# Masks of an attention pass: POOL selects on the probabilities in place of matmuls on the scores, and the products of a unit one step later

## The chip, the core and the metric

One NeuronCore of one Trainium2 chip runs the whole program. The metric is the device time of one execution in microseconds (us), median of three runs. The engines are TensorE (PE; PEld is its weight load), VectorE (DVE), ScalarE (ACT), GpSimd (POOL) and SyncE (SP, which issues the DMAs). Each engine runs its own instructions in their written order, and semaphores connect the engines.

## The reference

Four images of 128 channels and 32 x 32 positions pass through three stages. Only the second, attention over 1024 tokens with 16 heads, is touched by the change:

```python
def _attn(q, k, v, mask=None):
    s = jnp.einsum('bhqd,bhkd->bhqk', q, k) / np.float32(np.sqrt(HD))
    if mask is not None:
        s = jnp.where(mask, s, jnp.float32(-1000000000.0))
    return jnp.einsum('bhqk,bhkd->bhqd', jax.nn.softmax(s, -1), v)
...
o1 = _attn(q, k1, v1, causal[None, None])
...
o2 = _attn(q, ks, vs)                       # 256 selected keys, no mask
...
winmask = causal & (ii[:, None] - ii[None, :] < WINDOW)   # WINDOW = 64
o3 = _attn(q, kw, vw, winmask[None, None])
g = gate[:, :, None, None, None]
o = g[:, 0] * o1 + g[:, 1] * o2 + g[:, 2] * o3
```

The first stage is a non-local block (its own attention, with no mask), the third a mixture of eight experts, two of them kept for a token. Everything is float32.

## The kernel before

The attention part (`attention_part`, `turns`) goes through the four batches one after the other. A batch has 8 **sides** of 2 heads each, so there are 32 sides. Each side does two things at once.

**The exact pass** computes transposed scores (keys on the partitions, queries along the row), their exponentials, and the products with the values. It is cut into 25 **units**, each one block of 128 keys against up to 512 queries, in six groups (`SUMS`): branch 1 (selected keys, no mask), branch 2 (window), branch 1, branch 2, branch 0 (causal), branch 0, for the lower and upper 512 queries in turn. Their widths, units 0 to 24: 512 512 | 192 192 192 128 | 512 512 | 64 192 192 192 128 | 512 384 256 128 | 512 512 512 512 512 384 256 128. For each unit and head:

- PE, `scores`: two float32r matmuls (L1285, L1293) into one of three PSUM banks. Between them stands a bf16 matmul of the identity with a table of 0 and -8e9 where a mask is needed: `causal_k` (L1288, 128 columns, 8 units of branch 0) and `window_k` (L1291, the width of the unit, all 9 units of branch 2). Per side that is 16 and 18 mask matmuls.
- ACT: Exp from the bank into `prob` (L1342), a ring of four units (`PROBS`). The row maximum has been subtracted already by an extra row of the matmul.
- PE, `products`: four matmuls 32 columns wide per head pair and kind, side by side in the array (L1314), into one of two sum banks.
- After the last unit of a group ACT copies the sum banks into `products` and `sums` (L1351, L1353: step `sum`).

**The division** comes once for every two sides: in the odd ones (and, for the last group, at the start of the next even one) DVE takes reciprocals of `sums` in halves of 256 columns (L1386), POOL multiplies (L1365) and for branch 2 also adds (L1368). After the two causal groups PE issues `proj` (L1256, L1257), which waits for POOL's results.

**The preparation** of the next side lies between the units: 40 `max0`, `max1`, `max2` steps (PE matmuls L1221 to L1242 into three spare banks, DVE reductions L1395, L1400) and a few transposes.

`exact_pass` and `window` write one order of steps for all engines; each engine takes its own steps from it. Scores of unit u are followed, at every even u, by the products of units u-2 and u-1. POOL has only the division steps; they stand in its queue in the same order.

Of the kernel before, what the change touches and what calls it, by code (L numbers as in the profile page):

```python
# [10 lines left out]
BF16 = mybir.dt.bfloat16  # L11
ALU = mybir.AluOpType
# [3 lines left out]
P = 128  # L16
# [8 lines left out]
HP = HG // 2  # L25
# [4 lines left out]
KEEP, WINDOW = 256, 64  # L30
SCALE = 1.0 / 8.0
NE, HID = 8, 341
WN = P + WINDOW
LNE, RMSE = 1e-5, 1e-6
MASKED = -8.0e9
# [896 lines left out]
UNITS = units()  # L932
LAST = [max(u for u, x in enumerate(UNITS) if x[:2] == k) for k in SUMS]
LOCAL = LAST[3] + 1
SCORES = 3
SPARES = 3
PIECES = 2
# [12 lines left out]
def exact_pass(w):  # L950


    todo, pieces = [], []
    if w % 2 == 0 and w > 0:
        pieces = [("divide", w - 1, len(SUMS) - 1, piece) for piece in range(PIECES)] + [("proj", w - 1, 1)]
    for u in range(len(UNITS) + 1):
        if u < len(UNITS):
            todo.append(("scores", w, u))
        ready = range(u - 2, u) if u >= 2 and u % 2 == 0 else range(u - 1, u) if u == len(UNITS) else ()
        for done in ready:  # L960
            todo.append(("products", w, done))
        for done in ready:
            if done in LAST:
                k = LAST.index(done)
                todo.append(("sum", w, k))
                if w % 2 == 1 and (k < len(SUMS) - 1 or w == NSIDE - 1):
                    pieces += [("divide", w, k, piece) for piece in range(PIECES)]
                    if SUMS[k][0] == 0:
                        pieces.append(("proj", w, SUMS[k][1]))
        todo += pieces[:1]  # L970
        pieces = pieces[1:]
    return todo + pieces
# [63 lines left out]
def attention_part(nc, d, ps, ident, eps, sb):  # L1036
    m = Mem()
    m.ps, m.ident = ps, ident
    m.ident_bf = sb("ident_bf", [P, P], BF16)
    m.causal_q = sb("causal_q", [P, P], BF16)  # L1040
    m.causal_k = sb("causal_k", [P, P], BF16)
    m.window_q0 = sb("window_q0", [P, WN], BF16)
    m.window_q = sb("window_q", [P, WN], BF16)
    m.window_k = sb("window_k", [P, WN], BF16)
    m.plain = sb("plain", [P, VD])
    m.wproj = sb("wproj_g", [P, NG, C])
    m.wvp = sb("wvp_g", [P, NG, C])
    m.small = sb("maxima", [P, 128])
    m.t2 = sb("t2a", [C, T])
    m.gates = sb("gates_a", [P, 3])  # L1050
    m.q1a, m.q1b, m.qa, m.qb, m.kwa, m.kwb = [sb(n + "_s", [P, 2, HP, T], F32R)
                                              for n in ("q1a", "q1b", "qa", "qb", "kwa", "kwb")]
    m.ksa, m.ksb = [sb(n + "_s", [P, 2, HP, KEEP], F32R) for n in ("ksa", "ksb")]
    m.k1a, m.k1b = [sb(n + "_s", [P, 2, T], F32R) for n in ("k1a", "k1b")]
    m.v1 = sb("v1_s", [P, 2, NT, KVR])
    m.vw = sb("vw_s", [P, 2, NT, NW])
    m.vs = sb("vs_s", [P, 2, KEEP // P, NW])
    m.products = sb("products", [P, 3, T])
    m.sums = sb("sums", [P, 3, T])
    m.prob = sb("prob", [P, PROBS, HP, CH])  # L1060
    m.mrows = sb("mrows", [HP * NT, 3, P])

    attention_constants(nc, m, d)
    turns(nc, m, OPENING, None, Kept(d, 0))
    every = {k: d[k] for k in ("qh", "kwh", "ksh", "vwh", "vsh", "k1ah", "k1bh", "v1h", "gatesh", "t2")}
    with nc.Fori(0, B - 1) as b:
        turns(nc, m, MIDDLE, Kept({k: x[0:B - 1] for k, x in every.items()}, b),
              Kept({k: x[1:B] for k, x in every.items()}, b))
    turns(nc, m, CLOSING, Kept(d, B - 1), None)


def attention_constants(nc, m, d):

    stack = ExitStack()
    s = open_sems(nc, stack, "c_load c_zero_dve c_zero_pool")
    consts = [(m.ident_bf[:], "ident_bf"), (m.causal_q[:], "causal_q"), (m.causal_k[:], "causal_k"),
              (m.window_q0[:], "window_q0"), (m.window_q[:], "window_q"), (m.window_k[:], "window_k")]
    consts += [(m.wproj[:, g], d["wproj_g"][g]) for g in range(NG)]
    consts += [(m.wvp[:, g], d["wvp"][g]) for g in range(NG)]
    with nc.Block() as block:  # L1080
        @block.sync
        def _(sp):
            for dst, name in consts:
                sp.dma_start(dst, d[name] if isinstance(name, str) else name).then_inc(s["c_load"], 16)
            sp.wait_ge(s["c_load"], 16 * len(consts))

        @block.vector
        def _(dve):
            dve.memset(m.plain[:], 1.0)
            dve.memset(m.small[:], -3.0e38)  # L1090
            for x in (m.q1b, m.qb):
                dve.memset(x[HD:P].bitcast(F32), 0.0)
            dve.memset(m.ksb[HD:P].bitcast(F32), 0.0).then_inc(s["c_zero_dve"], 1)
            dve.wait_ge(s["c_zero_dve"], 1)
            dve.memset(m.ksb[HD:HD + 1].bitcast(F32), 1.0)

        @block.gpsimd
        def _(pool):
            for x in (m.k1b, m.kwb):
                pool.memset(x[HD:P].bitcast(F32), 0.0).then_inc(s["c_zero_pool"], 1)  # L1100
            pool.wait_ge(s["c_zero_pool"], 2)
            pool.memset(m.k1b[HD:HD + 1].bitcast(F32), 1.0)
            pool.memset(m.kwb[WROW:WROW + 1].bitcast(F32), 1.0)
    phase_end(nc, s)
    stack.close()
# [6 lines left out]
def turns(nc, m, plan, cur, nxt):  # L1112
# [3 lines left out]
    ps = m.ps  # L1116
    stack = ExitStack()
    s = open_sems(nc, stack, "t2_loaded gates_loaded stored near0 near1 keys0 keys1 far0 far1 late0 late1 "
                             "rows0 rows1 rows2 fill_ready emptied scores_ready exp_done products_done "
                             "banks_free inverse_done divided o_done max_done")  # L1120
    negs = [m.small[:, k * HP * NT:(k + 1) * HP * NT] for k in range(3)]
    partial = m.small[:, 64:64 + HP * NT * 2].rearrange("p (h t a) -> p h t a", h=HP, t=NT)
# [6 lines left out]
    with nc.Block() as block:  # L1129
# [73 lines left out]
        def _(pe):  # L1203
# [56 lines left out]
            def scores(side, u):  # L1260
# [13 lines left out]
                for h in range(HP):  # L1274
# [8 lines left out]
                        pe.wait_ge(s["exp_done"], turn - SCORES + 1)  # L1283
                    bank = ps[:, turn % SCORES, 0:w]
                    pe.matmul(bank, kx, qx[:, k, h, q0:q0 + w], start=True, stop=False, skip_group_check=True)  # L1285
                    at = q0 - j * P
                    if br == 0 and at == 0:
                        pe.matmul(bank[:, 0:P], m.ident_bf[:], m.causal_k[:], start=False, stop=False,  # L1288
                                  skip_group_check=True)
                    if br == 2:  # L1290
                        pe.matmul(bank, m.ident_bf[:], m.window_k[:, at:at + w], start=False, stop=False,  # L1291
                                  skip_group_check=True)
                    pe.matmul(bank, ky, qy[:, k, h, q0:q0 + w], start=False, stop=True, skip_group_check=True)\  # L1293
                        .then_inc(s["scores_ready"], 1)

            def products(side, u):
# [2 lines left out]
                n = side * len(UNITS) + u  # L1299
                k = side * len(SUMS) + SUMS.index((br, c))  # L1300
                first = u == 0 or u - 1 in LAST
                pe.wait_ge(s["exp_done"], HP * (n + 1))
                if first and k >= 2:
                    pe.wait_ge(s["banks_free"], k - 1)
                if side > 0 or br == 0:
# [48 lines left out]

        @block.gpsimd
        def _(pool):
            for step in plan.of(("divide",)):
                _, side, k, piece = step
                br, c = SUMS[k]
                w = CH // PIECES  # L1360
# [494 lines left out]
```

## Time and profile before

| | |
|---|---|
| median of 3 runs (lowest to highest) | 3072.85 us (3072.46 to 3079.17) |
| the profiled execution's own time | 3068.73 us |
| its span in the trace | 3066.9 us |
| mean granted PE clock | 0.921 |
| busy: PE, DVE, ACT, POOL | 85%, 59%, 44%, 21% |

The span runs from the first to the last instruction. A granted clock of 1.00 is 2.4 GHz. Ends of matmuls are modelled in the trace, so the distance from one matmul's start to the next one's says more than its duration. The exact pass runs from 794 to 2545 us of the span; a side takes 52.7 to 53.0 us there where no new batch begins.

### The profile page before, as it was taken

Reading aid. Unit: us, or ns where it says so; the run is one execution under the profiler, and the core shown is the slowest. Engines: PE = TensorE matmul, PEld = TensorE weight load, DVE = VectorE, ACT = ScalarE, POOL = GpSimd, SP = SyncE. Lnnn points to the kernel's source line nnn. Section 1 sums busy time; section 2 is a strip of 40 time slices with the busy share of each in tenths; the row PEclk is TensorE's granted clock in tenths of the full one; section 3 lists DMA queues with packets and bytes.
Section 4 is the critical chain, followed back from the end, with each engine's and each line's share of the span. In section 5 each row is a group of like instructions: output and inputs, shape, how many; then the busy total and the mean of one; then the engine's idle time right before and its main releaser. Section 6 shows DMA issues by size and latency. Waiting matters only on the chain. (4 is left out here: it accounts for less than half of the span.)

```text
span 3066.9 us, 48595 instructions
## 1 busy us (share of the span) xinstructions
PE 2601.3 (85%) x17280; PEld 1736.8 (57%) x17280; DVE 1813.7 (59%) x3117; ACT 1364.7 (44%) x2816; POOL 635.5 (21%) x607
## 2 busy tenths in 40 slices
PE   5666577663899999899997999997999993998999
PEld 3544445343566665566664666665666652777777
DVE  4755658474466566466555556654656644766755
ACT  2323333231355554455553555553555453544544
POOL 0331405043011011011001001101101112544445
PEclk9777788776799999999998999999999995999999
DMA  2451706257755655546565565654655602000000
GB/s 88 171 195 68 293 27 267 75 216 226 151 120 126 126 105 115 131 102 137 107 130 111 107 130 117 135 117 98 135 117 121 131 3 102 4 18 7 17 11 8
DMA packets 191886, 342.32 MB, mean 112 GB/s; under 512 B 65632, under 2 KB 95040, under 8 KB 191152
## 3 DMA queue, kind: packets, MB, share of 16 engines
q1 hardware_dynamic: 191664, 339.49, 43.8%
q8 instruction: 124, 2.03, 0.3%
q14 instruction: 98, 0.80, 0.1%
HBM read 224.56 MB, written 112.99 MB: 110 GB/s over the span
## 5 line engine op out<-in xcount | busy, mean ns | idle before, releaser
L1342 ACT ACTIVATE prob<-ps 128x512 f32<-128x512 f32 (+5 forms) x1600 | 636.8, 441 | 740.0 <-PE ps L1293 586.1
L1395 DVE TENSOR_REDUCE maxima<-ps 128x1 f32<-128x512 f32 (+3 forms) x768 | 387.4, 547 | 297.6 <-PE ps L1224 149.6
L1314 PE MATMUL ps<-prob,plain 128*32 128x512 f32 (+5 forms) x3200 | 512.0, 443 | 0.0
L1365 POOL TENSOR_TENSOR products<-products,sums 128x256 f32<-128x256 f32 x192 | 140.6, 732 | 1609.0 <-DVE sums L1386 1607.7
L1400 DVE TENSOR_REDUCE maxima<-ps 128x2 f32<-128x512 f32 (+1 forms) x512 | 294.4, 607 | 244.1 <-PE ps L1242 108.6
L1386 DVE RECIPROCAL sums<-sums 128x256 f32<-128x256 f32 x192 | 331.5, 1736 | 104.0 <-ACT sums L1353 104.0
L1285 PE MATMUL ps<-q1a_s,k1a_s 128*128 128x512 f32 (+3 forms) x768 | 303.2, 395 | 0.0
L1293 PE MATMUL ps<-q1b_s,k1b_s 128*128 128x512 f32 (+3 forms) x768 | 301.1, 393 | 0.0
L1314 PE MATMUL ps<-prob,v_s 128*32 128x512 f32 (+3 forms) x1536 | 284.3, 491 | 0.0
L1670 POOL TENSOR_TENSOR hl<-hid,hh 128x512 fp32r<-128x512 f32 x176 | 229.2, 1302 | 262.2 <-ACT hh L1614 257.8
L1221 PE MATMUL ps<-k1a_s,q1a_s 128*128 128x512 f32 (+3 forms) x768 | 234.6, 374 | 5.9 <-DMA k1a_s<-k1ah_dram 5.9
L1285 PEld LDWEIGHTS ps<-q1a_s,k1a_s 128*128 128x128 f32 x768 | 147.1, 192 | 126.8 <-issue 118.1
L1351 ACT ACTIVATE products<-ps,gates_a 64x512 f32<-64x512 f32 x192 | 130.9, 682 | 195.8 <-PE ps L1314 195.7
L875 POOL TENSOR_TENSOR rope<-turned 128x512 f32<-128x512 f32 (+1 forms) x80 | 93.9, 1174 | 507.7 <-DVE turned L903 505.4
L1755 DVE TENSOR_TENSOR mid<-ps,act_s 128x512 f32<-128x512 f32 x176 | 121.1, 688 | 131.8 <-PE ps L1548 116.4
L1285 PE MATMUL ps<-qa_s,kwa_s 128*128 128x192 f32 (+2 forms) x576 | 175.0, 304 | 19.6 <-ACT prob L1342 16.0
L1293 PE MATMUL ps<-qb_s,kwb_s 128*128 128x192 f32 (+2 forms) x576 | 184.1, 322 | 0.0
L1647 ACT ACTIVATE act_s<-ps 128x512 f32<-128x512 f32 x176 | 105.3, 599 | 174.7 <-PE ps L1548 172.9
L1285 PEld LDWEIGHTS ps<-qa_s,kwa_s 128*128 128x128 f32 x576 | 109.6, 190 | 98.5 <-issue 65.6
L1221 PEld LDWEIGHTS ps<-k1a_s,q1a_s 128*128 128x128 f32 x768 | 145.5, 196 | 24.3 <-DVE maxima L1395 8.6
L1240 PE MATMUL ps<-kwa_s,qa_s 128*128 128x192 f32 x512 | 125.9, 328 | 38.2 <-DMA kwa_s<-kwh_dram 38.2
L1293 PEld LDWEIGHTS ps<-q1b_s,k1b_s 128*128 128x128 f32 x768 | 151.4, 197 | 5.4
(300 smaller groups left out, 5623.2 us busy)
## 6 DMA issues: line engine op xcount, KB each, us to landing
qh_dram<-pairs SPq DMA_DIRECT2D x96, 512.0 KB, 3.7
kwh_dram<-pairs SPq DMA_DIRECT2D x64, 512.0 KB, 2.7
qa_s<-qh_dram SPq DMA_DIRECT2D x128, 256.0 KB, 4.3
kwa_s<-kwh_dram SPq DMA_DIRECT2D x128, 256.0 KB, 7.4
q1a_s<-qh_dram SPq DMA_DIRECT2D x128, 256.0 KB, 4.7
qb_s<-qh_dram SPq DMA_DIRECT2D x64, 256.0 KB, 9.1
kwb_s<-kwh_dram SPq DMA_DIRECT2D x64, 256.0 KB, 10.1
k1a_s<-k1ah_dram SPq DMA_DIRECT2D x32, 512.0 KB, 6.7
```

The lines of the kernel that those rows point to most:

```text
L1221: mm = pe.matmul(bank[:, 0:k1 - k0], m.q1a[:, k, h, i * P:(i + 1) * P], m.k1a[:, k, k0:k1], start=True, stop=True)
L1240: pe.matmul(bank[:, i * KEEP:i * KEEP + WN], m.qa[:, k, h, t * P:(t + 1) * P], m.kwa[:, k, h, k0:k0 + WN], start=True, stop=True, skip_gro ...
L1285: pe.matmul(bank, kx, qx[:, k, h, q0:q0 + w], start=True, stop=False, skip_group_check=True)
L1293: pe.matmul(bank, ky, qy[:, k, h, q0:q0 + w], start=False, stop=True, skip_group_check=True)\
L1314: mm = pe.matmul(ps[at:at + VD, SCORES + k % 2, q0 - c * CH:q0 - c * CH + w], w_, m.prob[:, n % PROBS, h, 0:w], start=first, stop=True, sk ...
L1342: act.activation(m.prob[:, u % PROBS, h, 0:w], ps[:, turn % SCORES, 0:w], ACT.Exp, scale=SCALE).then_inc(s["exp_done"], 1)
L1351: act.activation(m.products[rows, br, cc], ps[0:NW, SCORES + k % 2, :], ACT.Copy, scale=m.gates[0:NW, br:br + 1])
L1365: pool.tensor_tensor(o, o, m.sums[:, br, cc], ALU.mult).then_inc(s["divided"], 1)
L1386: dve.reciprocal(total, total).then_inc(s["inverse_done"], 1)
L1395: ins = dve.tensor_reduce(partial[:, h, i, part:part + 1], bank[:, 0:w], AX, ALU.max)
L1400: ins = dve.tensor_reduce(negs[1 if kind == "max1" else 2][:, at:at + 2], bank.rearrange("p (i n) -> p i n", i=2)[:, :, 0:w], AX, ALU.max, ...
L1670: pool.tensor_tensor(m.hl[:, n % RING, :], m.hid[:, n % RING, :], m.hh[:, n % RING, :].bitcast(F32), ALU.subtract).then_inc(s["lo_done"], 1)
```

## The change

The two tables `causal_k` and `window_k` and all 34 mask matmuls of a side are gone. Instead POOL sets the masked places of `prob` to zero after Exp, with `affine_select` for both heads at once: one select of 2 x 128 columns for the diagonal, one of 2 x 128 (2 x 64 for units 5, 8 and 12) for the window's far edge. Eight units of branch 2 get both, the second waiting for the first; unit 8 and the eight diagonal units of branch 0 get one: 25 selects a side. PE's products of such a unit wait for a new semaphore, `masked`, in place of `exp_done`. The products of a pair now come after the scores of an odd unit, one unit later than before.

```diff
+def masked_columns(unit):
+    br, c, j, q0, w = unit
+    return int(br == 2) + int(br != 1 and q0 == j * P)
+
+def masks(side, u):
+    return side * sum(masked_columns(x) for x in UNITS) + sum(masked_columns(x) for x in UNITS[:u + 1])
...
-        ready = range(u - 2, u) if u >= 2 and u % 2 == 0 else range(u - 1, u) if u == len(UNITS) else ()
+        ready = [u - 3, u - 2] if u >= 3 and u % 2 == 1 else []
+        if u == len(UNITS):
+            ready.append(u - 1)
...
-                    at = q0 - j * P
-                    if br == 0 and at == 0:
-                        pe.matmul(bank[:, 0:P], m.ident_bf[:], m.causal_k[:], start=False, stop=False,
-                                  skip_group_check=True)
-                    if br == 2:
-                        pe.matmul(bank, m.ident_bf[:], m.window_k[:, at:at + w], start=False, stop=False,
-                                  skip_group_check=True)
...
-                pe.wait_ge(s["exp_done"], HP * (n + 1))
+                if masked_columns(UNITS[u]):
+                    pe.wait_ge(s["masked"], masks(side, u))
+                else:
+                    pe.wait_ge(s["exp_done"], HP * (n + 1))
...
-            for step in plan.of(("divide",)):
+            for step in plan.of(("divide", "scores")):
+                if step[0] == "scores":
+                    _, side, u = step
+                    n = side * len(UNITS) + u
+                    br, c, j, q0, w = UNITS[u]
+                    own, at = m.prob[:, n % PROBS], q0 - j * P
+                    if masked_columns(UNITS[u]):
+                        pool.wait_ge(s["exp_done"], HP * (n + 1))
+                    if br != 1 and at == 0:
+                        pool.affine_select(own[:, :, 0:P], own[:, :, 0:P], [[0, HP], [1, P]], ALU.is_ge, 0.0,
+                                           base=0, channel_multiplier=-1).then_inc(s["masked"], 1)
+                    if br == 2:
+                        lo = max(0, WINDOW - at)
+                        if at == 0:
+                            pool.wait_ge(s["masked"], masks(side, u) - 1)
+                        pool.affine_select(own[:, :, lo:w], own[:, :, lo:w], [[0, HP], [-1, w - lo]], ALU.is_ge, 0.0,
+                                           base=WINDOW - 1 - at - lo, channel_multiplier=1).then_inc(s["masked"], 1)
+                    continue
```

**POOL's queue in an odd side.** Before, from the first division of a side to the first one of its fourth group:

```order
L1365 TENSOR_TENSOR products<-products,sums 128x256 x3
L1368 TENSOR_TENSOR products<-products 128x256
L1365 TENSOR_TENSOR products<-products,sums 128x256
L1368 TENSOR_TENSOR products<-products 128x256
L1365 TENSOR_TENSOR products<-products,sums 128x256 x3
```

Now, from the first half of the second group's division (L1391 is the multiplication, L1394 the addition, L1375 the diagonal's select, L1381 the window edge's) to the selects of unit 10:

```order
L1391 TENSOR_TENSOR products<-products,sums 128x256
L1394 TENSOR_TENSOR products<-products 128x256
L1381 AFFINE_SELECT prob<-prob 128x2x64
L1391 TENSOR_TENSOR products<-products,sums 128x256
L1394 TENSOR_TENSOR products<-products 128x256
L1375 AFFINE_SELECT prob<-prob 128x2x128
L1381 AFFINE_SELECT prob<-prob 128x2x128
L1391 TENSOR_TENSOR products<-products,sums 128x256
L1375 AFFINE_SELECT prob<-prob 128x2x128
L1381 AFFINE_SELECT prob<-prob 128x2x128
```

The select of unit 8 now stands between the two halves of the second division, those of unit 9 behind its second half, those of unit 10 behind the first half of the third.

**PE at the start of an even side.** Before: the last `max2` fill of unit 2, the products of units 0 and 1, `proj`, and the scores of unit 3:

```order
L1240 MATMUL ps<-kwa_s,qa_s 128x192
L1242 MATMUL ps<-window_q,ident_bf 128x192
L1314 MATMUL ps<-prob,vs_s 32x512 x2
L1314 MATMUL ps<-prob,plain 32x512 x2
L1314 MATMUL ps<-prob,vs_s 32x512 x2
L1314 MATMUL ps<-prob,plain 32x512 x2
L1256 MATMUL ps<-products,wvp_g 128x512
L1257 MATMUL ps<-products,wproj_g 128x512
L1285 MATMUL ps<-qa_s,kwa_s 128x192
```

Now `proj` (L1269, L1270), the scores of unit 3 (L1298, L1299), its fill, and then the first products (L1323):

```order
L1269 MATMUL ps<-products,wvp_g 128x512
L1270 MATMUL ps<-products,wproj_g 128x512
L1298 MATMUL ps<-qa_s,kwa_s 128x192
L1299 MATMUL ps<-qb_s,kwb_s 128x192
L1298 MATMUL ps<-qa_s,kwa_s 128x192
L1299 MATMUL ps<-qb_s,kwb_s 128x192
L1253 MATMUL ps<-kwa_s,qa_s 128x192
L1255 MATMUL ps<-window_q,ident_bf 128x192
L1253 MATMUL ps<-kwa_s,qa_s 128x192
L1255 MATMUL ps<-window_q,ident_bf 128x192
L1323 MATMUL ps<-prob,vs_s 32x512 x2
```

The products of units 0 and 1 have moved from ahead of `proj` to behind it, and the matmul between each pair of score matmuls is gone.

## Rows read from the trace of the kernel before

**Rows 1.** The page, busy time of each engine

```profile
PE 2601.3 (85%) x17280; PEld 1736.8 (57%) x17280; DVE 1813.7 (59%) x3117; ACT 1364.7 (44%) x2816; POOL 635.5 (21%) x607
```

**Rows 2.** One odd side, then the even one: us, busy time, PE clock, DMA

```profile
1281.00:1334.00 53.00, 52.12 (x437) 32.85 (x430) 37.70 (x54) 27.45 (x62) 10.26 (x14) 1.00 0.63 132
1334.00:1386.00 52.00, 50.62 (x424) 32.39 (x426) 26.84 (x47) 27.57 (x62) 1.46 (x2) 1.00 0.52 112
```

**Rows 3.** Groups by shape, mask matmuls: count | busy us, mean ns | idle before

```profile
L1288 PE MATMUL ps<-causal_k,ident_bf 128*128 128x128 bf16 x512 | 117.9, 230 | 0.0
L1291 PE MATMUL ps<-window_k,ident_bf 128*128 128x192 bf16 x384 | 98.5, 256 | 0.0
```

**Rows 4.** Timeline of PE: start, us; score matmuls and what follows them

```profile
1314.76 0.40 PE L1285 MATMUL ps<-q1a_s,k1a_s 128*128 128x512 f32 x1
...
1315.35 0.28 PE L1221 MATMUL ps<-k1a_s,q1a_s 128*128 128x256 f32 x1
...
1328.94 0.40 PE L1285 MATMUL ps<-q1a_s,k1a_s 128*128 128x512 f32 x1
...
1329.41 0.39 PE L1221 MATMUL ps<-k1a_s,q1a_s 128*128 128x512 f32 x1
...
1353.20 0.27 PE L1285 MATMUL ps<-qa_s,kwa_s 128*128 128x192 f32 x1
...
1353.53 0.27 PE L1240 MATMUL ps<-kwa_s,qa_s 128*128 128x192 f32 x1
...
1356.58 0.45 PE L1232 MATMUL ps<-ksa_s,qa_s 128*128 128x256 f32 x2
1356.86 0.40 PE L1285 MATMUL ps<-qa_s,ksa_s 128*128 128x512 f32 x1
```

**Rows 5.** Groups by shape, what POOL does

```profile
L1365 POOL TENSOR_TENSOR products<-products,sums 128x256 f32<-128x256 f32 x192 | 140.6, 732 | 1609.0 <-DVE sums L1386 1607.7
...
L1661 POOL MEMSET gn<- 128x1024 f32 x1 | 1.0, 957 | 7.8 <-POOLq L46 7.8
```

**Rows 6.** Timelines of ACT, DVE and POOL in an odd side, groups one to three

```profile
1297.28 0.68 ACT L1351 ACTIVATE products<-ps,gates_a 64x512 f32<-64x512 f32 x1 [1.98 <-PE ps L1314]
1304.12 0.68 ACT L1351 ACTIVATE products<-ps,gates_a 64x512 f32<-64x512 f32 x1 [0.70 <-PE ps L1314]
...
1300.66 1.74 DVE L1386 RECIPROCAL sums<-sums 128x256 f32<-128x256 f32 x1
...
1305.42 1.75 DVE L1386 RECIPROCAL sums<-sums 128x256 f32<-128x256 f32 x1 [0.83 <-ACT sums L1353]
...
1308.42 3.34 DVE L1386 RECIPROCAL sums<-sums 128x256 f32<-128x256 f32 x2
...
1300.41 0.73 POOL L1365 TENSOR_TENSOR products<-products,sums 128x256 f32<-128x256 f32 x1 [77.65 <-DVE sums L1386]
...
1308.06 0.73 POOL L1368 TENSOR_TENSOR products<-products 128x256 f32<-128x256 f32 x1
...
1311.04 0.73 POOL L1368 TENSOR_TENSOR products<-products 128x256 f32<-128x256 f32 x1
```

**Rows 7.** Timeline of PE between the products of that side

```profile
1303.64 0.28 PE L1314 MATMUL ps<-prob,vw_s 128*32 128x128 f32 x2
...
1303.98 0.50 PE L1285 MATMUL ps<-qa_s,ksa_s 128*128 128x512 f32 x1
...
1305.61 0.19 PE L1285 MATMUL ps<-qa_s,kwa_s 128*128 128x64 f32 x1
...
1310.88 0.25 PE L1314 MATMUL ps<-prob,vw_s 128*32 128x64 f32 x2
```

**Rows 8.** Timelines of PE and POOL around `proj` in an even side

```profile
1348.28 0.62 PE L1314 MATMUL ps<-prob,vs_s 128*32 128x512 f32 x2
...
1351.11 1.10 PE L1256 MATMUL ps<-products,wvp_g 128*128 128x512 f32 x2 [0.91 <-DVE maxima L1400]
...
1350.28 0.72 POOL L1365 TENSOR_TENSOR products<-products,sums 128x256 f32<-128x256 f32 x1 [2.26 <-DVE sums L1386]
```

More of the change, by code:

```diff
@@ L1040, in attention_part @@
     m.causal_q = sb("causal_q", [P, P], BF16)
-    m.causal_k = sb("causal_k", [P, P], BF16)
     m.window_q0 = sb("window_q0", [P, WN], BF16)
     m.window_q = sb("window_q", [P, WN], BF16)
-    m.window_k = sb("window_k", [P, WN], BF16)
     m.plain = sb("plain", [P, VD])
@@ L1075, in attention_constants @@
     s = open_sems(nc, stack, "c_load c_zero_dve c_zero_pool")
-    consts = [(m.ident_bf[:], "ident_bf"), (m.causal_q[:], "causal_q"), (m.causal_k[:], "causal_k"),
-              (m.window_q0[:], "window_q0"), (m.window_q[:], "window_q"), (m.window_k[:], "window_k")]
+    consts = [(m.ident_bf[:], "ident_bf"), (m.causal_q[:], "causal_q"),
+              (m.window_q0[:], "window_q0"), (m.window_q[:], "window_q")]
     consts += [(m.wproj[:, g], d["wproj_g"][g]) for g in range(NG)]
@@ L1118, in turns @@
     s = open_sems(nc, stack, "t2_loaded gates_loaded stored near0 near1 keys0 keys1 far0 far1 late0 late1 "
-                             "rows0 rows1 rows2 fill_ready emptied scores_ready exp_done products_done "
+                             "rows0 rows1 rows2 fill_ready emptied scores_ready exp_done masked products_done "
                              "banks_free inverse_done divided o_done max_done")
@@ L1794 @@
     arrays["causal_q"] = np.where(b <= a, 0, MASKED).astype(bfloat16)
-    arrays["causal_k"] = np.where(a <= b, 0, MASKED).astype(bfloat16)
     arrays["window_q0"] = np.where((w <= a) & (a - w < WINDOW), 0, MASKED).astype(bfloat16)
     arrays["window_q"] = np.where((w > a) & (w <= a + WINDOW), 0, MASKED).astype(bfloat16)
-    arrays["window_k"] = np.where((w >= a) & (w - a < WINDOW), 0, MASKED).astype(bfloat16)
     freq = 1.0 / 10000.0 ** (np.arange(0, 2 * HALF, 2, dtype=np.float32) / (2 * HALF))
```

## The prediction

> **What bounds the kernel now.** I read the busy times first: PE 85% of the span, POOL 21% [rows 1]. Then the windows of two neighbouring sides: PE is busy 52.1 of 53 us in an odd side and 50.6 of 52 in an even one, at full clock, while DVE goes from 37.7 to 26.8 us and POOL from 10.3 to 1.5 [rows 2]. Eleven us less on DVE don't shorten a side, so PE's own queue sets the time, and POOL has over 40 us free in each. What matters is (a) how much PE time the masks take, and (b) whether the selects are ready when PE wants them. For (b) the mean load of POOL says little: POOL works in order, and its divisions wait for DVE.
>
> **What is removed.** 34 mask matmuls a side, 1088 in all. Their modelled durations, 230 and 256 ns [rows 3], overlap their neighbours, so I take start-to-start distances [rows 4]. A head of 512 columns takes 1315.35 - 1314.76 = 0.59 us with its mask, and 1329.41 - 1328.94 = 0.47 without: 0.12 saved. A head of 192 columns takes 0.33 with its mask. No unmasked pair of that width exists; two matmuls of 256 columns take 0.28 [rows 4], which bounds the saving from below at 0.05. Following the slope from 256 to 512 columns ((0.47 - 0.28) / 256 per column) down to 192 gives 0.23 and a saving of 0.10. I take 0.12 for the 4 masks beside 512 columns and 0.10 for the other 30: 3.5 us a side, times 32 = **112 us**. Bounds: 34 x 0.12 x 32 = 131 above; 0.05 for the 30 gives 1.98 x 32 = 63 below. The two loads of the tables at the start are left out; they are once 80 KB.
>
> **What is added on POOL.** 25 selects a side. The trace has no select. From below, a memset of 1024 columns takes 957 ns, so 256 columns take 0.24 us or more, and 0.4 from start to start is my lower end [rows 5]. The nearest row with an input is the two-input multiplication of the same 256 elements: 0.73 [rows 5]. A select reads one input but makes an index and compares; I take 0.65, and 0.07 for the semaphore between two of them: **0.72 from start to start**, and 0.4 for the 2 x 64 ones. Nothing excludes more than the multiplication; 1.2 us is my upper end. In an even side POOL has nothing else: 25 x 0.72 = 18 us of 52, and the longest run is units 9 to 12, 8 selects or 5 us against over 7 us between PE's scores of unit 9 and its products of unit 12. There the masks are hidden, as they are by the extra unit of delay; from about 1 us a select they are not.
>
> **Where selects queue behind divisions** (16 odd sides). I follow the queue of POOL against the clock of the trace.
>
> - *Unit 5.* Group 0's sum starts at 1297.28 on ACT; call it 0. POOL's first multiplication ends at 3.9 (1300.41 + 0.73), then unit 4's two selects to 5.3; DVE's second reciprocal ended at 5.1, its multiplication lasts to 6.1, unit 5's selects to 7.2. Before, PE came to unit 5 at 1303.64, 6.4 after 0 [rows 7]. Now unit 3's scores and fill (two heads of 0.33 and a fill of some 0.3: 1.0) stand ahead of 0, unit 7's with three fills (1305.61 - 1303.98 = 1.63) come in between [rows 7], and 0.4 of masks are saved: 6.6. Wait **0.5**.
> - *Unit 9.* Group 1's sum starts at 1304.12: 0 again [rows 6]. The division's first half ends at 4.7 (1308.06 + 0.73). Unit 8's select ends at 5.1. The second reciprocal, which in the old order had two fills ahead of it, can now follow the first at once and ends near 4.8; POOL then multiplies and adds to 6.7, and unit 9's selects end at 8.15. Before, PE reached unit 8's products at 1310.88, 6.9 us after unit 7's scores began [rows 7]; less unit 7 (1.63), plus unit 11 with its fill (1.0), less 0.8 of masks: 5.5. Unit 8 is ready then, unit 9 is wanted at 5.75. Wait **2.4**.
> - *Unit 11.* The third group's first half to 8.9, unit 10's selects to 10.35 (wanted near 10.6), second half to 11.1, unit 11's selects to 12.55; wanted near 11.0. Wait **1.5**.
>
> Behind PE's waiting product stand its own next scores and fills, so ACT and DVE starve with it and nothing is made up. Later selects (units 13 to 16, 21 to 24) are single ones and clear. Sum 4.4 us, times 16 = **70 us**. With 0.4 from start to start the same walk gives 0, 1.7 and 1.0 = 2.7 (43 us), with 0.81 it gives 0.9, 2.7 and 1.9 = 5.5 (88), with 1.2 about 10 (160), and then even sides wait 3 us too (48).
>
> **What is moved.** `proj` at the start of an even side waits for POOL's last half division, which ends at 1351.00 (1350.28 + 0.72); PE stood 0.91 us before it, having spent 1348.28 to 1350.2 on the products of units 0 and 1 [rows 8]. That cover now stands behind `proj`, and the division does not come earlier. PE waits some 1.9 us more, and unit 2's 0.2 us of saved masks are lost in the wait too: 2.0 x 12 (sides 2, 4 and 6 of four batches) = **24 us**. The other `proj` keeps its cover. Moving products later gives nothing back elsewhere: PE shows almost no wait for Exp ahead of products, and the three score banks are freed as before.
>
> **Sum.** -112 + 70 + 24 = -18 us on the profiled execution's 3068.7 (its span is 3066.9, the rest lies around it). That execution is 4.1 under the median of the runs, so in terms of the median the forecast is **3055**.
>
> **A rule against it.** The POOL additions at 1308.06 and 1311.04 each last 0.73, as alone, though DVE's two reciprocals ran from 1308.42 to 1311.76 [rows 6]: the second even began inside one. So a select beside a reciprocal costs nothing in my sum. The Trainium skill ("SBUF — State Buffer", section "SBUF: two separate sides") says that DVE and GpSimd share one port pair, which a GpSimd operation, or a DVE operation in a two-port mode or with two SBUF inputs, takes for its whole length, and the other then blocks fully. These rows show no block between a reciprocal and an addition; a select is not among them.
>
> The Trainium skill ("GPSIMD Engine Reference", 3.1) gives 1.8 cycles an element at 1.2 GHz as GpSimd's best case; an estimate from that page is 0.38 us for 256 elements, and the sum by it would be near 3030. No row here shows it.
>
> **Rivals.**
> - *The cover holds* (0.16). POOL and DVE run ahead of my walk, or PE is later at each point, and only `proj` costs: -112 + 24 = -88, 2985. For it: POOL's low load [rows 2]. Against it: the walk to unit 9 rests on reciprocals of 1.74 us that can't be had sooner.
> - *The select is slow* (0.30), the case on the other side: from about 0.8 us start to start the sum reaches zero (-112 + 88 + 24); at 1.2 it is -112 + 160 + 48 + 24 = +120, 3193. For it: generic code that builds an index may well cost more than a multiplication; against it, one input instead of two.
> - *Selects and reciprocals block each other* (0.12): each of the two latest units waits one more reciprocal, 1.74 x 2 x 16 = 56 on top of the sum, 3111. Against it the overlap above.
> - *Forecast* (0.42): masks cheap, odd sides wait 2.7 to 5.5 us; 3025 to 3090 (savings of 0.10 to 0.12 at either end).
>
> **Chances.** A measurement of this kernel can tell 0.3%, 9 us, from no change. Faster: 0.27 of the forecast's share and all of the first rival, 0.43. Same: 0.12, most of it the forecast's upper part. Slower: 0.07 of the forecast, 0.27 of the slow select, 0.11 of the blocking, 0.45. The range runs from half of the first rival, 2990, to near the slow select's 1.2 us, 3190.
>
> **What will show it.** The select's group: mean near 0.65; over 0.9 the slow rival holds. Distance of heads: 0.47 for all of 512 columns, 0.23 for 192. PE's idle time ahead of products (L1323) with POOL's select as its end: none in even sides, some 4.4 us in odd ones, mostly at unit 9; if it is small, the cover held. `proj` at the start of sides 2, 4, 6: a wait near 2.9 us. Sides, 52.7 to 53.0 us before: sides 2, 4 and 6 near 51.5, odd ones near 54. If DVE's reciprocals grow longer than 1.74, or selects show two lengths, the engines block each other. What would make me wrong most easily is the select's length, and next a third limit, DVE's reductions, becoming the odd side's bound once PE is quicker.

## The result, and the profile after

The changed kernel takes 3137.24 us (median of 4 runs, 3134.17 to 3139.01), the kernel before 3074.56 beside it (4 runs, 3072.46 to 3079.17). The ratio is 1.0201, with a 95% interval of 1.0183 to 1.0218: **2% slower**. The forecast was 3055, with 0.43 on faster. The range held the time, but the direction was wrong, and so, as will be seen, was the reason given for a slower one. The profiled execution has a span of 3137.3 us and a mean granted clock of 0.910 (0.921 before).

The page's busy times of the changed kernel answer to [rows 1]:

```profile
PE 2563.5 (82%) x16192; PEld 1693.2 (54%) x16192; DVE 1812.8 (58%) x3117; ACT 1348.2 (43%) x2816; POOL 938.9 (30%) x1407
```

PE does 38 us less and stands idle more: 574 us of the span, where it was 466. So the time was lost in waits. The windows of an odd side (it starts at 1311.6) and an even one (1478.6), in the columns of [rows 2]:

```profile
1311.00:1366.00 55.00, 50.23 (x395) 30.86 (x394) 38.54 (x55) 26.91 (x62) 19.58 (x39) 1.00 0.55 117
1478.00:1533.00 55.00, 49.43 (x412) 31.28 (x404) 26.50 (x48) 27.84 (x64) 11.16 (x27) 1.00 0.55 117
```

Before, PE lacked 0.9 us of 53 and 1.4 of 52; now 4.8 and 5.6 of 55. For every kernel below I give the mean length of a side, worked out from the trace as the distance between the starts of two sides' first score matmuls: the 12 odd sides that don't end a batch, the 12 even ones that don't begin one, the 4 that begin one, and the 3 that end one with the next batch's preparation behind them. Before: 52.9, 52.7, 54.3 and 70.8 us. After: 55.0, 55.6, 52.7 and 74.3, together 12 x 2.1 + 12 x 2.9 - 4 x 1.6 + 3 x 3.5 = 64 us.

What the selects cost, in the groups by shape of POOL:

```profile
L1375 POOL TENSOR_SCALAR_AFFINE_SELECT prob<-prob 128x256 f32<-128x256 f32 x512 | 208.9, 408 | 828.1 <-ACT prob L1351 828.1
L1391 POOL TENSOR_TENSOR products<-products,sums 128x256 f32<-128x256 f32 x192 | 140.1, 730 | 438.3 <-DVE sums L1412 437.3
...
L1381 POOL TENSOR_SCALAR_AFFINE_SELECT prob<-prob 128x128 f32<-128x128 f32 x96 | 28.4, 295 | 90.2 <-ACT prob L1351 85.9
```

A select takes 408 ns, not the 650 assumed. PE's waits over the attention part (800 to 2560 us) are sums over all sides: waited for, us in total, times, longest. Of the kernel before, and of the changed one:

```profile
PE ps L1285 <- ACT prob L1342: 21.1, 57, 3.0
PE ps L1256 <- DVE maxima L1400: 10.9, 12, 0.9
```

```profile
PE ps L1298 <- ACT prob L1351: 64.4, 96, 1.4
PE ps L1269 <- DVE maxima L1426: 33.1, 12, 2.8
...
PE ps L1298 <- DMA qb_s<-mrows: 10.8, 14, 1.1
PE ps L1234 <- DVE maxima L1421: 8.9, 15, 0.6
PE ps L1234 <- DVE maxima L1426: 6.9, 13, 0.9
PE ps L1269 <- DVE maxima L1421: 6.0, 15, 0.4
PE ps L1245 <- DVE maxima L1426: 4.7, 15, 0.3
PE ps L1323 <- POOL prob L1381: 4.4, 10, 0.4
```

Products (L1323) wait 4.4 us for selects over the whole attention part, where I had put 70. New or longer are the waits of scores for Exp (L1298 for ACT), of `proj` (L1269, put down to DVE's maxima, which had long been done: below, the real releaser is POOL), of scores for the rows of maxima that a DMA brings, and of the fills (L1234, L1245) for DVE. Fills are PE's preparation matmuls into the spare banks; the rows of maxima are what the extra row of the score matmuls holds. All of these waits belong to the order of the steps, not to the masks. The timeline at the start of that even side shows the largest, first PE, then DVE and POOL:

```profile
1483.72 0.26 PE L1255 MATMUL ps<-window_q,ident_bf 128*128 128x192 bf16 x1
1486.74 1.10 PE L1269 MATMUL ps<-products,wvp_g 128*128 128x512 f32 x2 [2.76 <-DVE maxima L1426]
...
1484.09 1.74 DVE L1412 RECIPROCAL sums<-sums 128x256 f32<-128x256 f32 x1
...
1485.91 0.72 POOL L1391 TENSOR_TENSOR products<-products,sums 128x256 f32<-128x256 f32 x1 [2.26 <-DVE sums L1412]
```

PE waits 2.76 us for POOL's half division, which ends at 1486.63; in [rows 8] it waited 0.91. That is the 1.9 us that the prediction named.

### The profile page after: what moved, and what is told of

Its sections match the earlier page's. It is cut to its first block and busy times, and to the rows that moved or that the text cites. A ratio compares the mean times of both kernels' runs of the same rounds, so it can differ in the third digit from the quotient of the medians.

```text
span 3137.3 us, 47229 instructions
## 1 busy us (share of the span) xinstructions
PE 2563.5 (82%) x16192; PEld 1693.2 (54%) x16192; DVE 1812.8 (58%) x3117; ACT 1348.2 (43%) x2816; POOL 938.9 (30%) x1407
## 5 line engine op out<-in xcount | busy, mean ns | idle before, releaser
L1351 ACT ACTIVATE prob<-ps 128x512 f32<-128x512 f32 (+5 forms) x1600 | 620.1, 440 | 796.6 <-PE ps L1299 641.2
L1323 PE MATMUL ps<-prob,plain 128*32 128x512 f32 (+5 forms) x3200 | 527.2, 450 | 0.0
L1375 POOL TENSOR_SCALAR_AFFINE_SELECT prob<-prob 128x256 f32<-128x256 f32 x512 | 208.9, 408 | 828.1 <-ACT prob L1351 828.1
L1412 DVE RECIPROCAL sums<-sums 128x256 f32<-128x256 f32 x192 | 331.9, 1739 | 143.1 <-ACT sums L1362 143.1
L1298 PE MATMUL ps<-q1a_s,k1a_s 128*128 128x512 f32 (+3 forms) x768 | 293.1, 390 | 0.1
L1323 PE MATMUL ps<-prob,v_s 128*32 128x512 f32 (+3 forms) x1536 | 284.2, 491 | 0.0
L1391 POOL TENSOR_TENSOR products<-products,sums 128x256 f32<-128x256 f32 x192 | 140.1, 730 | 438.3 <-DVE sums L1412 437.3
L1234 PE MATMUL ps<-k1a_s,q1a_s 128*128 128x512 f32 (+3 forms) x768 | 243.1, 380 | 24.1 <-DVE maxima L1421 8.9
L1299 PE MATMUL ps<-q1b_s,k1b_s 128*128 128x512 f32 (+3 forms) x768 | 259.9, 346 | 0.0
L1298 PE MATMUL ps<-qa_s,kwa_s 128*128 128x192 f32 (+2 forms) x576 | 176.9, 326 | 63.8 <-ACT prob L1351 63.8
L1298 PEld LDWEIGHTS ps<-q1a_s,k1a_s 128*128 128x128 f32 x768 | 146.8, 191 | 130.6 <-issue 92.9
L1298 PEld LDWEIGHTS ps<-qa_s,kwa_s 128*128 128x128 f32 x576 | 112.4, 195 | 157.2 <-ACT prob L1351 79.8
L1234 PEld LDWEIGHTS ps<-k1a_s,q1a_s 128*128 128x128 f32 x768 | 146.1, 196 | 59.5 <-DVE maxima L1421 31.8
L1299 PEld LDWEIGHTS ps<-q1b_s,k1b_s 128*128 128x128 f32 x768 | 145.9, 190 | 14.7 <-issue 3.8
```

The costliest lines, as they stand in the source:

```text
L1234: mm = pe.matmul(bank[:, 0:k1 - k0], m.q1a[:, k, h, i * P:(i + 1) * P], m.k1a[:, k, k0:k1], start=True, stop=True)
L1323: mm = pe.matmul(ps[at:at + VD, SCORES + k % 2, q0 - c * CH:q0 - c * CH + w], w_, m.prob[:, n % PROBS, h, 0:w], start=first, stop=True, sk ...
L1351: act.activation(m.prob[:, u % PROBS, h, 0:w], ps[:, turn % SCORES, 0:w], ACT.Exp, scale=SCALE).then_inc(s["exp_done"], 1)
L1375: pool.affine_select(own[:, :, 0:P], own[:, :, 0:P], [[0, HP], [1, P]], ALU.is_ge, 0.0, base=0, channel_multiplier=-1).then_inc(s["masked" ...
L1391: pool.tensor_tensor(o, o, m.sums[:, br, cc], ALU.mult).then_inc(s["divided"], 1)
L1412: dve.reciprocal(total, total).then_inc(s["inverse_done"], 1)
```

## Experiments

The theory after the result was: **the later place of the products costs the time, and the selects are hidden**. The rival was the prediction's own: PE waits for selects that queue behind divisions.

### Masks and place taken apart

Four kernels separate the two halves of the change. The first keeps the mask matmuls and only moves the products:

```diff
-        ready = range(u - 2, u) if u >= 2 and u % 2 == 0 else range(u - 1, u) if u == len(UNITS) else ()
+        ready = [u - 3, u - 2] if u >= 3 and u % 2 == 1 else []
+        if u == len(UNITS):
+            ready.append(u - 1)
```

> The kernel before with one edit: the products of a pair come after the scores of an odd unit, one unit later. Mask matmuls stay, no selects. Theory W (PE waits for selects that queue behind POOL's divisions): only the lost cover of the projection costs, 12 x 2 us, so about 3098 us. Theory D (the later place of the products is itself the loss: the cover of the projection, fills that wait for DVE in odd sides, scores that wait for Exp): about 3115 to 3140 us.

Measured: 3186.98 us (3182.06 to 3188.18), ratio 1.0364 [1.0344, 1.0383]. Moving alone costs 112 us, more than either theory expected.

The second is the changed kernel with that edit undone: selects, products in their old place.

> The changed kernel with the products back in their old place, after the scores of an even unit: selects on POOL, no mask matmuls. W: selects are wanted a unit sooner, so the waits grow, 3150 us or more. D: the loss is gone and part of the 112 us of masks comes back, 3010 to 3080 us; even sides may show short waits for selects of branch 2.

Measured: 3176.86 us (3170.13 to 3181.0), ratio 1.0329 [1.0303, 1.0355]. That is the time which the rival expected for this kernel, not the theory's. Even sides are 50.9 us, better than any so far; odd ones are 60.8. The reason stands in the waits of PE:

```profile
PE ps L1321 <- POOL prob L1379: 66.3, 61, 1.7
...
PE ps L1321 <- POOL prob L1373: 27.3, 15, 1.8
```

And in the timelines of one odd side, POOL, DVE and PE (L1389 is the multiplication, L1410 the reciprocal):

```profile
1329.47 0.72 POOL L1389 TENSOR_TENSOR products<-products,sums 128x256 f32<-128x256 f32 x1 [4.12 <-DVE sums L1410]
1330.14 0.41 POOL L1373 TENSOR_SCALAR_AFFINE_SELECT prob<-prob 128x256 f32<-128x256 f32 x1
1330.62 0.41 POOL L1379 TENSOR_SCALAR_AFFINE_SELECT prob<-prob 128x256 f32<-128x256 f32 x1
...
1327.63 1.75 DVE L1410 RECIPROCAL sums<-sums 128x256 f32<-128x256 f32 x1 [2.63 <-ACT sums L1360]
...
1331.08 0.36 PE L1321 MATMUL ps<-prob,vw_s 128*32 128x192 f32 x2 [1.72 <-POOL prob L1379]
```

POOL stands 4.12 us before a multiplication that waits for DVE, with two selects of 0.41 behind it, and PE waits for the second. That is the mechanism of the prediction, word for word, but in the kernel without the delay: 93.6 us of such waits here, 4.4 in the changed one. The clock adds to it. These are the windows of one odd side and of the even one behind it:

```profile
1319.28:1378.67 59.39, 51.98 (x395) 32.48 (x396) 38.74 (x55) 26.77 (x62) 19.53 (x39) 0.94 0.52 109
1378.67:1429.48 50.81, 48.69 (x401) 30.69 (x397) 26.36 (x47) 26.92 (x63) 11.18 (x27) 1.00 0.60 127
```

Over the 12 odd sides that don't end a batch the granted clock is 0.92; length times what the clock lacks of 1.00 comes to 58 us there, and to nothing in the even sides.

The third and the fourth have no masks at all in the exact pass (neither matmuls nor selects; the masking of the transposed scores is left out of the computation), with products late and in the old place:

```diff
-                if masked_columns(UNITS[u]):
-                    pe.wait_ge(s["masked"], masks(side, u))
-                else:
-                    pe.wait_ge(s["exp_done"], HP * (n + 1))
+                pe.wait_ge(s["exp_done"], HP * (n + 1))
...
-            for step in plan.of(("divide", "scores")):
+            for step in plan.of(("divide",)):
```

> The changed kernel without any select: the masks of the exact pass are left out altogether (the causal and window masks are missing from the result), products wait for Exp alone, in the late place. W: the changed kernel less its waits for selects, 3060 to 3070 us. D: the selects were hidden, so still 3120 to 3135 us.

Measured: 3136.78 us (3127.25 to 3141.59), ratio 1.0194 [1.0166, 1.0223], the time of the changed kernel. With the delay, 800 selects cost nothing that can be told.

> As the run before it (the masks of the exact pass left out altogether), but with the products in their old place: what the mask matmuls cost at most. If PE's queue alone bounds a side, 3074 - 112 = 2962 us. If the rows of the next side, which are sent behind its loads, land at P12 + 21 us and bound the even sides (they landed 1.6 us ahead of the side's end before), at most about 1.8 us of each even side can be saved, and the time is near 2990 to 3010 us.

Measured: 3010.57 us (3004.04 to 3017.47), ratio 0.9782 [0.9760, 0.9803]. So the masks' matmuls are worth 3075.45 - 3010.57 = 65 us in the old place and 3186.98 - 3136.78 = 50 in the later one, and the later place costs 126 us without masks and 112 with them. Either way round the two make +61, and the changed kernel measured +63: since its selects add nothing to the third kernel's time, the theory holds for it and the rival falls.

Why 65 and no more: the matmuls' own time went down by more. PE's score steps of the 12 odd sides, from a unit's first score matmul to whatever follows its last, fall from 23.4 to 20.8 us a side, and the waits for Exp inside them rise from 0.5 to 1.2; without these waits they fall by 3.3 us, and in even sides by 3.2. The fills of odd sides take 0.85 us longer. PE's waits in the fourth kernel, where the one before had 21.1 us for Exp and none for fills:

```profile
PE ps L1296 <- ACT prob L1346: 41.7, 82, 2.7
...
PE ps L1243 <- DVE maxima L1421: 2.8, 15, 0.2
PE ps L1232 <- DVE maxima L1416: 2.5, 15, 0.2
```

What stays open is which of the waits make up the 126.

### What the later place is made of

**Rows of maxima.** The wait for the DMA stands at the end of even sides, ahead of the next side's first scores (timeline of PE, changed kernel, end of the side from 1478.6):

```profile
1531.98 0.28 PE L1263 MATMUL ps<-ident,maxima 128*16 128x128 f32 x1
...
1533.07 0.50 PE L1298 MATMUL ps<-qa_s,ksa_s 128*128 128x512 f32 x1 [0.81 <-DMA qb_s<-mrows]
```

In SP's queue the rows stand behind the loads of the side after (`local`), and these wait for unit 12's products, now issued later. This edit lets the rows of the first two branches go first:

```diff
                 whole(side)
+                row(side, 2)
+                row(side, 1)
                 if ("local", side + 1) in plan.loads:
                     local(side + 1)
-                for br in (2, 1, 0):
-                    row(side, br)
+                row(side, 0)
```

> The changed kernel with one edit in SP's queue: the rows of maxima of groups 2 and 1 of the next side are sent ahead of the loads of the side after it, not behind them. If the late products hold back those loads (they wait for unit 12) and the rows behind them hold back the next side, the 1.0 us at the end of each of 12 even sides goes: near 3125 us. If the rows are not what the sides wait for: 3137 us, as before the edit.

Measured: 3124.18 us (3120.91 to 3132.66), ratio 1.0163 [1.0129, 1.0198]; even sides 54.6, odd ones 55.4. The DMA's row is gone from the waits. It was worth 3137 - 3124 = 13 us.

**`proj` at the start of even sides**, put one step later, so that the products of units 0 and 1 cover its wait again:

```diff
-        pieces = [("divide", w - 1, len(SUMS) - 1, piece) for piece in range(PIECES)] + [("proj", w - 1, 1)]
+        pieces = [("divide", w - 1, len(SUMS) - 1, piece) for piece in range(PIECES)] + [None, ("proj", w - 1, 1)]
...
-        todo += pieces[:1]
+        todo += [x for x in pieces[:1] if x]
```

> The changed kernel with the projection at the start of an even side one unit later, so behind the first two products again. Lost cover as a cause: 12 x 1.85 us, and the slow clock behind the long wait with it (0.4 to 0.8 us each), come back: 3105 to 3115 us. If the wait only moves elsewhere: 3130 to 3137 us.

Measured: 3074.82 us (3070.81 to 3079.33, 10 runs), ratio 1.0002 [0.9988, 1.0017]: the whole loss is gone with one step moved by one place. It was worth 62 us, where `proj`'s wait is 33.1 in the changed kernel, 22 above before. PE around `proj` in this kernel:

```profile
1460.19 0.60 PE L1323 MATMUL ps<-prob,vs_s 128*32 128x512 f32 x2
...
1460.83 1.10 PE L1269 MATMUL ps<-products,wvp_g 128*128 128x512 f32 x2
```

There is no wait. Even sides fall from 55.6 to 50.9: 4.7 us, of which the gap ahead of `proj` is 2.8. The means of the steps show the rest: the score steps of units 3 and 5 behind it become 0.7 us shorter each, that of unit 4 0.3 longer, `proj` itself and the fills 0.4 shorter each. Unit 5's is its wait for an Exp, here 0.50 us in the changed kernel:

```profile
1493.15 0.33 PE L1298 MATMUL ps<-qa_s,kwa_s 128*128 128x128 f32 x1 [0.50 <-ACT prob L1351]
```

With `proj` behind the products, ACT has them done by then. Part of unit 3's has only moved to unit 4; the other part and `proj`'s are the clock, in 7 of the 12 sides. One of them in windows of the changed kernel, columns as above: the wait for `proj`, then a stretch behind it:

```profile
1371.50:1374.30 2.80, 0.04 (x1) 0.03 (x1) 2.31 (x3) 0.00 (x0) 0.82 (x2) 1.00 1.01 212
1376.30:1377.30 1.00, 1.00 (x6) 0.83 (x4) 0.59 (x1) 0.15 (x1) 0.00 (x0) 0.50 1.12 221
```

PE had next to nothing to do for 2.80 us, and soon after ran at a granted clock of 0.50, its lower level of 1.2 GHz. Unit 3's step takes 1.2 to 1.6 us in these 7 sides and 0.82 in the other 5, where the clock stayed at 1.00. Length times what the clock lacks of 1.00 comes to 15 us over the 12 even sides here and to nothing with `proj` put back; in the first experiment it is 22 of the 112 us. So of the 62 us 33 are the wait itself, up to 15 the clock and 9 unit 5's step.

Odd sides have such stretches as well, and `proj` has no part in them: 7 us over 12 sides in both kernels. One is this:

```profile
1438.00:1441.00 3.00, 2.20 (x30) 1.57 (x26) 1.77 (x3) 2.16 (x6) 0.00 (x0) 0.93 0.02 5
1441.00:1444.00 3.00, 3.00 (x16) 0.47 (x16) 2.75 (x3) 0.00 (x0) 2.24 (x4) 0.50 0.00 0
```

The products in that stretch (timeline, first row) against those at full clock (second row):

```profile
1440.88 1.07 PE L1323 MATMUL ps<-prob,vs_s 128*32 128x512 f32 x2
...
1330.41 0.60 PE L1323 MATMUL ps<-prob,vs_s 128*32 128x512 f32 x2
```

**Scores behind ACT's copies.** ACT's two copies of the sum banks stand ahead of the Exps of units 4, 8 and 10 now (of 3, 7 and 9 before), and PE's scores of units 5, 9 and 11 wait for those Exps. This edit puts the copies behind the next unit's Exps in ACT's queue:

```diff
-            for step in plan.steps:
+            acts = [x for x in plan.steps if x[0] in ("scores", "sum")]
+            for n in range(len(acts) - 2, -1, -1):
+                if acts[n][0] == "sum" and acts[n + 1][0] == "scores":
+                    acts[n], acts[n + 1] = acts[n + 1], acts[n]
+            for step in acts:
```

> The changed kernel with ACT's two copies of a sum moved behind the Exp of the unit that follows. If scores (units 5, 9 and 11) wait since Exp stands behind those copies on ACT, 1.5 us a side comes back: near 3090 to 3105 us. If DVE's reciprocals, which now start later, are the tighter limit in odd sides, only even sides gain: 3115 to 3135 us.

Measured: 3259.96 us (3256.76 to 3264.13), ratio 1.0596 [1.0564, 1.0628]. PE's waits:

```profile
PE ps L1234 <- DVE maxima L1425: 70.4, 28, 2.7
PE ps L1323 <- POOL prob L1385: 33.1, 22, 2.0
...
PE ps L1298 <- ACT prob L1355: 3.8, 2, 2.5
```

The scores' wait for Exp falls from 64.4 to 3.8 us, and even sides from 55.6 to 54.4. But odd sides go from 55.0 to 64.4: the sums reach DVE later, so its reciprocals do, and the fills and selects behind them; the granted clock of odd sides is 0.91 with it, where it was 0.99. Neither of the two expected times came: this order costs more than it saves. What the wait for Exp is worth alone, this run doesn't tell.

**DVE's reciprocals** in odd sides. Here DVE inverts 8 of every 256 columns only (the division of the others is left out of the computation):

```diff
-                    dve.reciprocal(total, total).then_inc(s["inverse_done"], 1)
+                    dve.reciprocal(total[:, 0:8], total[:, 0:8]).then_inc(s["inverse_done"], 1)
```

> The changed kernel with every reciprocal on DVE cut to 8 of its 256 columns (the division of the other columns is left out), so some 0.1 to 0.2 us in place of 1.74. If the odd sides (54.9 us) are long because fills find their spare banks not emptied while DVE works on reciprocals, they come down by 2 to 3 us, to about 52.5; and the projection at the start of even sides, which waits for two reciprocals, no longer leaves PE 2.8 us idle: in all 16 x 2.5 + 12 x 4 = 88 us less, near 3050 us. If DVE is not what odd sides wait for, only the projection's part comes back: near 3090 us.

Measured: 3005.39 us (2999.54 to 3011.73), ratio 0.9779 [0.9757, 0.9801]. Odd sides fall from 55.0 to 50.2 us, even ones from 55.6 to 52.1 (the last division lies in them, ahead of `proj`). The time is 45 us below the one expected, and an odd side is no longer than the 51.2 us that it takes without masks in the old place, with whole reciprocals. No run has short reciprocals in the old place, so this doesn't show that nothing is left of the delay's cost there. In the changed kernel the same stretch reads, DVE, then PE:

```profile
1322.96 1.74 DVE L1412 RECIPROCAL sums<-sums 128x256 f32<-128x256 f32 x1
1324.61 1.82 DVE L1426 TENSOR_REDUCE maxima<-ps 128x2 f32<-128x512 f32 x3
...
1325.89 1.10 PE L1245 MATMUL ps<-ksa_s,qa_s 128*128 128x256 f32 x4 [0.31 <-DVE maxima L1426]
...
1329.31 0.36 PE L1298 MATMUL ps<-qa_s,kwa_s 128*128 128x192 f32 x1 [0.80 <-ACT prob L1351]
```

A fill finds its spare bank full while DVE catches up after a reciprocal, and soon after a score step waits for Exp. The run with short reciprocals parts the two. No wait of a fill for DVE is left in it, but scores wait for Exp as long as before:

```profile
PE ps L1298 <- ACT prob L1351: 66.9, 101, 1.5
```

In the 12 odd sides this wait is 1.97 us a side in the changed kernel and 1.96 with short reciprocals, while PE's fills become 2.8 us a side shorter. So what made odd sides long is mainly DVE, busy with reciprocals when a fill wants its bank emptied, and not the wait for Exp.

### Selects without the delay

If the queue on POOL is what spoils the old place, the queue can be changed instead. From the second kernel above, POOL alone takes the divisions of the first five groups later, between the selects:

```diff
+            held, queue = [], []
+            place = {0: 6, 1: 13, 2: 15, 3: 17, 4: 18}
...
+                if step[0] == "divide" and step[2] in place and (step[1] < NSIDE - 1 or step[2] < 4):
+                    held.append(step)
+                    continue
+                queue.append(step)
+                if step[0] == "scores":
+                    due = [x for x in held if step[2] >= place[x[2]] + x[3] or step[2] >= 19]
+                    queue += due
+                    held = [x for x in held if x not in due]
```

> Selects on POOL with the products in their old place, and POOL's multiplications of groups 0 to 4 moved back in POOL's queue to where their reciprocals are long done (behind unit 6, and one half a unit from unit 13 on). If the 102 us between this kernel without that edit and the kernel before come from selects that stand behind a multiplication which waits for DVE, 8 to 9 us of each of 16 odd sides come back: 3177 - 140 = 3037 us. If the selects are late by their own length (two of 0.4 us after each Exp), nearly nothing changes: 3160 to 3177 us.

Measured: 3022.39 us (3016.42 to 3025.13), ratio 0.9821 [0.9790, 0.9851]. This edit of one queue takes 154 us off the second kernel; odd sides are 51.5, even ones 50.8. The granted clock is 1.00 in all the odd sides that had 0.92, so the 154 us are for the most part the waits for selects, 87 us less, and the clock that had gone down with them, up to 58. PE's waits at the place of the 93.6 us:

```profile
PE ps L1321 <- POOL prob L1391: 6.8, 33, 0.5
```

Then both repairs, rows first and `proj` one step later, on the changed kernel, on the kernel before and on this one (the edits are those above):

> The changed kernel with both repairs, the rows ahead of the loads and the projection behind the first products: 3137 - 62 - 13 = 3062 us if they add up. If the sides that gained from one are those that gain from the other, 3070 to 3075 us. What stays against the kernels with products in their old place is then the waits for Exp and for DVE.

> The kernel before with the same two edits (mask matmuls, products in the old place): the projection's wait of 0.9 us before it goes in 12 sides, the rows did not bind: 3074 - 11 = 3063 us; 3074 if the 0.9 us come back elsewhere.

> Selects on POOL, products in the old place, POOL's multiplications moved back in its queue (3022 us so far), and the same two edits: 0.3 us at the end and 0.9 us before the projection in each of 12 even sides go: 3008 us. If the loads or DVE bound the even sides otherwise: 3020 us.

| with both repairs | us (lowest to highest) | ratio to before | odd, even side |
|---|---|---|---|
| changed kernel | 3069.63 (3065.09 to 3079.70) | 0.9987 [0.9976, 0.9998] | 55.2, 49.9 |
| kernel before | 3064.35 (3057.48 to 3067.66) | 0.9965 [0.9954, 0.9975] | 52.9, 51.8 |
| selects in the old place | 3017.37 (3005.08 to 3017.91) | 0.9804 [0.9778, 0.9829] | 51.5, 49.8 |

The repairs give the kernel before 9 us and the changed one 68, so for the most part they mend what the delay broke. For the selects in the old place they do nothing that can be told: the intervals with them and without (0.9790 to 0.9851) overlap. At equal repairs the changed kernel still takes 3069.6 - 3017.4 = 52 us more than the one with products in the old place and divisions moved in POOL's queue, and 12 x (55.2 - 51.5) = 44 of them lie in odd sides. Over the attention part PE waits 23.2 us for DVE ahead of fills in place of 5.1, and 60.4 in place of 42.3 for Exp. That the first is the part that counts is argued from the run with short reciprocals. The best kernel that computes the reference is about 2% faster than before: the selects pay once POOL's queue is re-ordered, the delay that came with them doesn't.

## Why the prediction was wrong, by its steps

- **The step that failed**: "Moving products later gives nothing back elsewhere". I meant it as "costs nothing elsewhere" too: the delay's only price was `proj`, 24 us. It measured 112 us with mask matmuls and 126 without. I had asked of the moved products only what they had covered, not who waits for their end: ACT's copies and DVE's reciprocals of the sums, and the loads on SP's queue behind which the rows stand.
- **`proj` unprotected, 24 us.** The wait came out as said, 2.76 us against "near 2.9", and as a wait it adds 33.1 - 10.9 = 22 us. But giving the cover back took off 62: scores behind it met unfinished Exps, and stretches behind it ran at the lower clock (up to 15 us). The mechanism was right, its followers were left out.
- **Masks, -112 us.** The matmuls' own time was read rightly; it was wrong to take all of it as time of the kernel. The pair of 192 columns without a mask takes 0.22 to 0.23 us from its start to a fill behind it, against 0.33 with its mask [rows 4], so the 0.10 was right:

```profile
1491.63 0.28 PE L1298 MATMUL ps<-qa_s,kwa_s 128*128 128x192 f32 x1
...
1491.86 0.28 PE L1253 MATMUL ps<-kwa_s,qa_s 128*128 128x192 f32 x1
```

  PE's score steps gave up 3.2 to 3.3 us a side without their waits, 104 us in all, and 65 of these came: some 21 us went back to waits for Exp, 5 to waits of fills for DVE, and where the last 13 went isn't shown. DVE is the third limit named last in the prediction. That 65 is near its lower bound of 63 is luck: the bound came from a saving of 0.05, which isn't what happened.
- **Selects behind divisions, +70 us.** 4.4 us measured. The select was faster (0.48 start to start for 0.72), but even at 0.4 my walk still gave 43. It followed POOL against a PE clock of before that was too early at units 5 and 9, the largest wait. At unit 9, from ACT's copy at 1327.74 on, POOL's selects ended after 7.3 us (8.15 in the walk), and PE came to unit 8's products after 6.55 (5.5 in the walk), having waited 0.80 and 0.67 us for Exps on its way; what was left is 0.45, not 2.4:

```profile
1327.74 0.68 ACT L1360 ACTIVATE products<-ps,gates_a 64x512 f32<-64x512 f32 x1 [1.71 <-PE ps L1323]
1334.29 0.25 PE L1323 MATMUL ps<-prob,vw_s 128*32 128x64 f32 x2
...
1335.06 0.36 PE L1323 MATMUL ps<-prob,vw_s 128*32 128x192 f32 x2 [0.45 <-POOL prob L1381]
```

  At unit 11 PE came when the walk said, and POOL was ready by then. In the old place the mechanism is the largest cost of all, 94 us of waits and up to 58 of clock, and a re-ordered queue removes it. The delay cures it too; it is only the dearer cure.
- **The rivals.** "The cover holds" was right on the selects, and its sum was short of the delay's cost by some 100 us and long on the masks by 47, so it said 2985. "The select is slow" ended on the right side for a wrong reason: 0.41 us. "Selects and reciprocals block each other" is not seen: the select at 1323.40 below runs wholly inside the reciprocal from 1322.96 to 1324.70 and takes its 0.41, and reciprocals keep their mean of 1739 ns (1736 before). The 97 selects of 256 elements that ran wholly inside a reciprocal took 409 ns in the mean, the 598 that met none 408.

```profile
1323.40 0.41 POOL L1375 TENSOR_SCALAR_AFFINE_SELECT prob<-prob 128x256 f32<-128x256 f32 x1
```

The Trainium skill ("SBUF — State Buffer", section "SBUF: two separate sides") has a DVE operation take the shared port pair in a two-port mode or with two SBUF inputs; a reciprocal of one float32 input is neither where it runs in an ordinary mode, and by that reading the trace agrees. The Trainium skill ("GPSIMD Engine Reference", 3.1) with its best case of 1.8 cycles gave an estimate of 0.38 us for a select of 256 elements; the trace has 0.408, so that page was nearer than the row of the multiplication that I chose.

## What to carry to other kernels

When a step is moved later on the engine that sets the time, price its end as well as its cover: list every queue in which someone waits for it (here ACT's copies, DVE's reciprocals behind them, and the DMA queue), and what stands behind each waiter. When work is given to an engine with free time, look at what its queue waits for, not at its load; another order in that queue can be the cheap cure (154 us here) where a delay on the bound engine is a dear one (112 to 126 us lost). And try such a change in its halves, since here a gain of 2% was hidden under a loss of 4%.

## What was not expected of the hardware

- GpSimd's `affine_select` takes 408 ns for 128 x 256 float32 elements and 295 for 128 x 128: from these two, 0.88 ns an element and some 0.18 us fixed. The two-input multiplication of the same 256 takes 730.
- A mask matmul of 128 or 192 columns in a stream of score matmuls takes about 3.3 / 34 = 0.10 us of PE's time, less than half of its modelled 230 to 256 ns.
- Waits of PE came with a lower clock. After a stretch in which PE was busy 2.20 of 3 us the granted clock was 0.50 for the next 3, and a group of products took 1.07 us in place of 0.60. No product of 512 columns lasted over 0.8 in the kernel before. With 94 us of waits for selects the odd sides ran at 0.92, without them at 1.00.
